# Scanning two states per instruction in a fused selective-scan and expert-FFN kernel

## Chip, cores and metric

The kernel runs on 1 core of one Trainium2 chip. The metric is the device time of one execution in microseconds; the median of several executions counts, lower is better.

## What is computed

For each of B=4 sequences of L=512 positions, with 512 channels and 16 states n, a selective scan is computed and added to x, and then a feed-forward part is added to that. Cut to what matters here (`silu`, the projections and the router left out):

```python
def step(state, inp):                      # over the 512 positions
    d, b, c, u = inp
    dA = jnp.exp(d[..., None] * A)         # [channel, state]
    state = state * dA + (d * u)[..., None] * b[:, None, :]
    y = jnp.einsum('bdn,bn->bd', state, c) # sum over the 16 states
    return (state, y)
...
y = y + D[None, :, None] * x
y = y * silu(z)                            # z = layernorm(x)
x = x + y
x = x + ffn(layernorm(x))                  # shared expert + top 2 of 16 experts
```

## The kernel before

One program with hand-placed instructions on five engines, ordered by semaphores. It has three stages. A preparation stage (to about 105 us) makes u, dt, B, C and silu(z) and stores them in scratch memory. The **scan stage** (105 to 580 us) is the one that the change touches. Then comes the routed part of the feed-forward, 47 units of 128 rows, which the change touches only in which PSUM banks some tiles have.

The scan stage has 16 **slots**: batch b = 0..3 times channel tile q = 0..3 (128 channels on partitions, 512 positions along the free dimension). Slots of batch 0 are written out; batches 1 to 3 are a loop of three turns whose body is the four slots. For each of the 16 states n a slot does:

- ScalarE (`decay`, L912): exp(dt*A[n]) into a PSUM bank of a ring of three, HS = banks 0 to 2; it waits until the bank is free (three states back).
- GpSimd (L1151): dbu = B * (dt*u), four states in one instruction of 2048 elements, made one slot ahead. dbu has one buffer, so each group of four waits for the scan of that group in the slot before.
- VectorE (`scan`, L1332): tensor_tensor_scan over the 512 positions, in place in the bank, or into h_p for the four states of POOL_N.
- product with C: on VectorE (`times_c`, L1346), bank to gs (ring of 6), for 12 states; on GpSimd (`times_c`, L1159), h_p to g_p, for the 4 states of POOL_N = (1, 5, 9, 13). VectorE's order is scan n, then the product of state n-1, so that between a scan and its product another scan runs.
- TensorE (`y_sum`, L615): turns the product (four 128x128 transposes) and adds it up in Y = bank 3, in the order of ORDER; the skip term m_du comes in the same way.

When the 16 states (and the skip term) of a slot are summed, VectorE multiplies Y with silu(z) into bank 7 (`take_y`, L1360, at state 2 of the next slot) and adds x (`gated`, L1367, at state 4); SyncE stores the result and at the end of a batch the rows are loaded again as xt.

Slots of batches 1 to 3 also carry one 128-row tile of the batch before through layernorm, router and shared expert ("rows"): `stats` on VectorE (L1374, at state 8 for q=0, 1 otherwise; three instructions that depend on each other), `rstd` on GpSimd (L1175), `xn` on ScalarE (L949), `xn_turn` on TensorE (L631, into TP = bank 7), `xnT_copy` on ScalarE (L955, after decay 15), `router` and the pieces of `shared` (L639, L647: 4+4 pieces of gate and up rows, 2 turns, 6 pieces of down), `gate` and `hT_copy` on ScalarE, `hidden` on VectorE (L1384), `swish` on GpSimd (L1169), `row_out` on ScalarE (L964). The tables at L41 to L52 say after which state each is issued; every engine takes its own instructions strictly in that order. GpSimd's slot is: m_w = dt*u, then four times (product with C of one state of the slot before, dbu of a group), swish after the first, rstd at the end.

Of the kernel before, what the change touches and what calls it, by code (L numbers as in the profile page):

```python
# [12 lines left out]
P = 128  # L13
# [41 lines left out]
def last_in_bank(k):  # L55

    if k >= RING_H:
        return k - RING_H
    return max(m for m in range(STEPS) if m % RING_H == k) - STEPS
# [12 lines left out]
def program(nc, x, ctxT, inT, convw, convb, xpT, dtT, dtb, alog, dskip, gateT, wgu, wdn, sgu, sdn, out):  # L72
# [11 lines left out]
    with ExitStack() as stack:  # L84
# [7 lines left out]
        bank = [stack.enter_context(nc.psum_tensor(f"bank{i}", [P, 512], F32)) for i in range(8)]  # L92
# [6 lines left out]
        TX, TH, ROUNDED = bank[3], bank[7], bank[0:3]  # L99
# [442 lines left out]
        def _(pe):  # L542
# [72 lines left out]
            def y_sum(b, q, m):  # L615

                i, n = b * DT + q, ORDER[m]
                if m == 0 and not (isinstance(i, int) and i < 1):
                    pe.wait_ge(y_taken, i)
                if m == SKIP_AT:  # L620
                    pe.wait_ge(du_ready, i + 1)
                    add_turned(m_du, False, False)
                if n in POOL_N:
                    pe.wait_ge(gp_ready, i * NP + by_pool(n) + 1)
                    tile = g_p[:, by_pool(n) % RING_P, :]
                else:
                    pe.wait_ge(g_ready, i * NV + by_vector(n) + 1)
# [3 lines left out]
            def xn_turn(j, x1_count):  # L631
                pe.wait_ge(xn_ready, j[0] + 1)
                pe.wait_ge(x1_ready, x1_count)
                pe.wait_ge(xnT_copied, 1 + j[0])
                for t in range(KH):
                    last = nc.tensor.transpose(TP[:, t * P:(t + 1) * P], f_xn[:, j[1] % 2, t * P:(t + 1) * P], ident[:])
                last.then_inc(xnT_ready, 1)
# [55 lines left out]
            def slot(b, q, rows):  # L693
# [12 lines left out]
                for n in range(NS):  # L706
                    y_sum(b, q, n)
                    for piece in early[PE_AT[n]:PE_AT[n + 1]] + late[LATE_AT[n]:LATE_AT[n + 1]]:
                        piece()
                    if rows and n == XN_TURN_AT[q > 0]:  # L710
                        xn_turn(f, i)
# [19 lines left out]
            for q in range(TB - 1):  # L731
                xn_turn((first + q, q), B * DT)
                router((first + q, q), first + q + 1, first + 2)
            whole((first + 2, 2), NT - 1)
            xn_turn((NT - 1, TB - 1), B * DT)
# [106 lines left out]
        def _(act):  # L842
# [69 lines left out]
            def decay(b, q, n):  # L912

                k = q * NS + n
                if not (isinstance(b, int) and b == 0 and k < RING_H):
                    m = last_in_bank(k)
                    if m % NS in POOL_N:
                        act.wait_ge(scan_done, b * STEPS + m + 1)
                    else:
                        act.wait_ge(g_ready, (b * DT + m // NS) * NV + by_vector(m % NS) + 1)  # L920
                if isinstance(b, int) and b == 0 and k == 2:
                    act.wait_ge(xd_copied, B)
                if n == 0:
                    act.wait_ge(d_loaded[q % 2], b * 32 + (q // 2) * 16 + 16)
                f(HS[k % RING_H][:], m_dt[:, q % 2, :], ACT.Exp, scale=c_a[:, q, n:n + 1]).then_inc(exp_done, 1)  # L925
# [29 lines left out]
            def xnT_copy(j, past):  # L955
                act.wait_ge(xnT_ready, 1 + j[0] + 1)
                act.wait_ge(down_ready, 1 + past)
                f(f_xnT[:, j[1], :], TP[:], ACT.Copy).then_inc(xnT_copied, 1)
# [9 lines left out]
            def slot(b, q, rows):  # L968
                j = ((b - 1) * DT + q, q)
                first = isinstance(b, int) and b == 0 and q == 0  # L970
                for n in range(NS):
# [24 lines left out]
                    if rows and n == XNT_AT[q > 0]:  # L996
                        xnT_copy(j, j[0])
# [21 lines left out]
            def xnT_of(q):  # L1019
                xnT_copy((first + q, q), first + q - 1)  # L1020
# [82 lines left out]
        def _(pool):  # L1103
# [28 lines left out]
            def slot(b, q, rows):  # L1132
# [7 lines left out]
                for gr in range(NG):  # L1140
# [3 lines left out]
                    else:  # L1144
                        times_c(*((b, q - 1) if q else (b - 1, DT - 1)), POOL_N[gr])
# [13 lines left out]
            def times_c(b, q, n):  # L1159

                i, at = b * DT + q, by_pool(n)
                pool.wait_ge(scan_done, i * NS + n + 1)
                pool.wait_ge(c_loaded[n // GRP], b * 16 + 16)
                if not (isinstance(i, int) and i == 0 and at < RING_P):
                    j, m = (i, POOL_N[at - RING_P]) if at >= RING_P else (i - 1, POOL_N[at - RING_P + NP])
                    pool.wait_ge(ymm_done, j * NS + ORDER.index(m) + 1)
                g.tensor_tensor(g_p[:, at % RING_P, :], h_p[:, at % RING_P, :], Cs[:, n, :], ALU.mult).then_inc(gp_ready, 1)  # L1167
# [21 lines left out]
            for n in POOL_N:  # L1189
                if n == POOL_N[SWISH_AFTER + 1]:  # L1190
# [68 lines left out]
        def _(dve):  # L1259
# [72 lines left out]
            def scan(b, q, n):  # L1332
                k = q * NS + n
                if n % GRP == 0:
                    dve.wait_ge(dbu_ready, (b * DT + q) * NG + n // GRP + 1)
                dve.wait_ge(exp_done, b * STEPS + k + 1)
                h = HS[k % RING_H][:]
                to = h
                if n in POOL_N:
                    i, at = b * DT + q, by_pool(n)  # L1340
                    if not (isinstance(i, int) and i == 0 and at < RING_P):
                        dve.wait_ge(gp_ready, i * NP + at - RING_P + 1)
# [3 lines left out]
            def times_c(b, q, n):  # L1346
                k, i, at = q * NS + n, b * DT + q, by_vector(n)
                dve.wait_ge(scan_done, b * STEPS + k + 1)
                if n % GRP == 0:
                    dve.wait_ge(c_loaded[n // GRP], b * 16 + 16)  # L1350
                if isinstance(i, int) and i == 0 and at < RING_G:
                    dve.wait_ge(z_turned, TB * (B - 1))
                    dve.wait_ge(dtp_ready, DT * (B if at >= RING_G - 2 else B - 1))
                else:

                    j, m = (i, DVE_N[at - RING_G]) if at >= RING_G else (i - 1, DVE_N[at - RING_G + NV])
                    dve.wait_ge(ymm_done, j * NS + ORDER.index(m) + 1)
                v.tensor_tensor(gs[:, (q * NV + at) % RING_G, :], HS[k % RING_H][:], Cs[:, n, :], ALU.mult).then_inc(g_ready, 1)  # L1358

            def take_y(b, i, q, copied):  # L1360

                dve.wait_ge(ymm_done, (i + 1) * NS)
                dve.wait_ge(xnT_copied, 1 + copied)
                dve.wait_ge(s_loaded[q % 2], b * 32 + (q // 2) * 16 + 16)
                v.tensor_tensor(TP[:], Y[:], m_szT[:, q % 2, :], ALU.mult).then_inc(y_taken, 1)

            def gated(b, i, q):  # L1367
# [4 lines left out]
                v.tensor_tensor(m_x[:, par], m_x[:, par], TP[:].rearrange("p (t j) -> p t j", t=TB), ALU.add).then_inc(x1_ready, 1)  # L1372

            def stats(j, jb):  # L1374
                at = j[1]
                dve.wait_ge(xt_loaded[at], jb * 16 + 16)
                v.bn_stats(f_st[:, at, :], xt[:, at, :]).then_inc(tstat_done, 1)
                dve.wait_ge(tstat_done, j[0] * 2 + 1)
                held(dve)
                v.bn_aggr(f_mv[:, at, :], f_st[:, at, :]).then_inc(tstat_done, 1)  # L1380
                dve.wait_ge(tstat_done, j[0] * 2 + 2)
                v.tensor_scalar(f_ve[:, at:at + 1], f_mv[:, at, 1:2], EPS, None, ALU.add).then_inc(var_ready, 1)

# [17 lines left out]

            def slot(b, q, rows):
                i = b * DT + q
                later = not (isinstance(b, int) and b == 0 and q == 0)
                j = ((b - 1) * DT + q, q)
                for n in range(NS):
                    scan(b, q, n)
                    if isinstance(b, int) and b == 0:
                        if q == 0 and n == SOFT_AT:
                            for k in range(DT):  # L1410
                                soft(B - 1, k)
                        if q == 0 and n in GAP_AT:
                            gap(B - 1, GAP_AT.index(n))
                        if q == 0 and n - 1 in GAP_AT:
                            total(B - 1, GAP_AT.index(n - 1))
                        if q == 2 and n == CLEAR_AT:
                            clear()
                    if n and n - 1 in DVE_N:
                        times_c(b, q, n - 1)
                    if n == TAKE_AT and later:  # L1420
                        take_y(*((b, i - 1, q - 1) if q else (b - 1, i - 1, DT - 1)), i - DT if rows else 0)
                    if n == GATED_AT and later:
                        gated(*((b, i - 1, q - 1) if q else (b - 1, i - 1, DT - 1)))
                    for c in range(2):
                        if n == HIDDEN_AT[c]:
# [4 lines left out]
                    if rows:  # L1430
                        if n == STATS_AT[q > 0]:
                            stats(j, b - 1)
                times_c(b, q, NS - 1)

            for q in range(DT):
# [4 lines left out]
            take_y(B - 1, B * DT - 1, DT - 1, NT - TB)  # L1440
# [9 lines left out]
            for q in range(TB - 1):  # L1450
                stats((first + q, q), B - 1)
            whole((first + 1, 1))
            stats((NT - 1, TB - 1), B - 1)
# [180 lines left out]
```

## Time and profile before

| | |
|---|---|
| runs | 1059.53, 1061.68, 1061.94 us; median 1061.68 us |
| profiled execution | 1053.36 us, its span 1051.6 us |
| busy over the span | PE 86%, DVE 79%, POOL 72%, ACT 49% |
| scan stage | about 105 to 580 us of the span |
| DVE in the scan stage | 28.8 of 29 us in most windows |
| TensorE's granted clock | 0.54 to 0.61 in the slots of batch 0, 1.00 in most of the loop |

The span runs from the first to the last instruction; the execution's own time is 1.8 us longer. In rows of the timeline the first number is the start, the second the duration, both in us; the difference between the starts of two neighbours is what the first one costs its engine.

### The profile page before, as it was taken

Reading aid. Unit: us, or ns where it says so; the run is one execution under the profiler, and the core shown is the slowest. Engines: PE = TensorE matmul, PEld = TensorE weight load, DVE = VectorE, ACT = ScalarE, POOL = GpSimd, SP = SyncE. Lnnn points to the kernel's source line nnn. Section 1 sums busy time; section 2 is a strip of 40 time slices with the busy share of each in tenths; the row PEclk is TensorE's granted clock in tenths of the full one; section 3 lists DMA queues with packets and bytes.
Section 4 is the critical chain, followed back from the end, with each engine's and each line's share of the span. In section 5 each row is a group of like instructions: output and inputs, shape, how many; then the busy total and the mean of one; then the engine's idle time right before and its main releaser. Section 6 shows DMA issues by size and latency. Waiting matters only on the chain.

```text
span 1051.6 us, 16598 instructions
## 1 busy us (share of the span) xinstructions
PE 899.8 (86%) x4352; PEld 653.7 (62%) x4353; DVE 828.9 (79%) x1349; ACT 517.5 (49%) x959; POOL 753.6 (72%) x482
## 2 busy tenths in 40 slices
PE   5876655689999789988999999869999999998993
PEld 2222334566665456655665555649998999887992
DVE  4788999999999899989999216768798989898000
ACT  3777634445655465555665222115554555454541
POOL 2436889899999799989993111027989888877872
PEclk9997656789999999999999989889999999999996
DMA  5568922562228322562210230134676777675432
GB/s 175 195 263 308 341 64 78 209 210 81 81 74 330 117 80 80 209 230 80 80 60 30 75 128 11 65 125 141 173 226 187 217 189 218 159 228 100 77 56 35
DMA packets 69987, 152.14 MB, mean 145 GB/s; under 512 B 7585, under 2 KB 23969, under 8 KB 64306
## 3 DMA queue, kind: packets, MB, share of 16 engines
q1 hardware_dynamic: 59410, 126.97, 35.2%
q0 software_dynamic: 10528, 24.65, 11.9%
q8 instruction: 14, 0.23, 0.1%
q14 instruction: 35, 0.29, 0.1%
HBM read 112.80 MB, written 38.80 MB: 144 GB/s over the span
## 4 chain that ended last, share of the span: by engine, by line
DVE 41%; PE 29%; issue 19%; DMA 3%; ACT 2%; DVEq 2%; POOL 1%; SPq 0%; POOLq 0%; ACTq 0%
DVE bank L1344 8%; PE bank L665 6%; DVE gs L1358 6%; PE bank L684 5%; DVE e_gu_lo L1571 4%; DVE e_gu_hi L1570 4%; PE bank L769 3%; PE bank L611 3%; PE bank L771 3%; DVE bank L1563 3%; PE bank L770 3%; DVE p_acc L1286 3%; DVE e_dn_lo L1571 2%; DVE e_dn_hi L1570 2%; DVE h_p L1344 2%
## 5 line engine op out<-in xcount | busy, mean ns | idle before, releaser
L1151 POOL TENSOR_TENSOR dbu<-bcs,m_w 128x2048 f32<-128x2048 f32 x64 | 296.1, 4627 | 11.4 <-DVE bank L1344 8.6
L925 ACT ACTIVATE bank<-m_dt,c_a 128x512 f32<-128x512 f32 x256 | 171.0, 686 | 196.8 <-DVE gs L1358 196.7
L1344 DVE TENSOR_TENSOR_SCAN bank<-bank,dbu 128x512 f32<-128x512 f32 x192 | 229.0, 1213 | 14.6 <-ACT bank L925 10.5
L611 PE MATMUL bank<-ident,gs 128*128 128x128 f32 x768 | 135.2, 307 | 70.0 <-DVE gs L1358 63.0
L665 PE MATMUL bank<-ws_gu,f_xnT 128*128 128x352 f32 x576 | 191.9, 474 | 2.8 <-ACT f_hT L947 1.9
L611 PEld LDWEIGHTS bank<-ident,gs 128*128 128x128 f32 x768 | 95.3, 154 | 129.5 <-DVE gs L1358 107.3
L665 PEld LDWEIGHTS bank<-ws_gu,f_xnT 128*128 128x128 f32 x576 | 106.2, 196 | 50.5 <-issue 5.3
L769 PE MATMUL bank<-e_gu_hi,e_xT_hi 128*128 x376 | 130.0, 346 | 4.0 <-DVEq L1585 3.1
L1358 DVE TENSOR_TENSOR gs<-bank,bcs 128x512 f32<-128x512 f32 x192 | 126.5, 665 | 0.0
L771 PE MATMUL bank<-e_gu_hi,e_xT_lo 128*128 x376 | 121.8, 324 | 0.0
L770 PE MATMUL bank<-e_gu_lo,e_xT_hi 128*128 x376 | 121.7, 324 | 0.0
L684 PE MATMUL bank<-ws_dn,f_hT 128*128 128x512 f32 (+1 forms) x216 | 107.3, 611 | 0.0
L1233 POOL DMA_INDIRECT out_rows<-e_y,t_tok x47 | 75.0, 1595 | 33.6 <-DMA out_rows<-e_y,t_tok 21.4
L1216 POOL TENSOR_TENSOR e_xT_lo<-e_xT,e_xT_hi 128x512 fp32r<-128x512 f32 x47 | 85.0, 1807 | 17.5 <-ACT e_xT_hi L1052 17.5
L1173 POOL TENSOR_TENSOR f_sg<-f_sg,f_g 128x352 f32<-128x352 f32 x36 | 33.7, 942 | 80.4 <-ACT f_sg L941 80.3
L1167 POOL TENSOR_TENSOR g_p<-h_p,bcs 128x512 f32<-128x512 f32 x64 | 81.6, 1274 | 10.0 <-DVE h_p L1344 6.3
L1563 DVE CAST bank<-e_gu 128x352 fp32r<-128x352 f32 x128 | 64.0, 521 | 22.7 <-issue 9.6
L1079 ACT ACTIVATE e_y<-bank,zero,t_w 128x512 f32<-128x512 f32 x47 | 36.7, 780 | 84.7 <-PE bank L771 83.0
L1344 DVE TENSOR_TENSOR_SCAN h_p<-bank,dbu 128x512 f32<-128x512 f32 x64 | 77.0, 1203 | 0.4 <-ACT bank L925 0.4
L769 PEld LDWEIGHTS bank<-e_gu_hi,e_xT_hi 128*128 128x128 f32 x376 | 71.3, 190 | 5.6 <-issue 5.6
L770 PEld LDWEIGHTS bank<-e_gu_lo,e_xT_hi 128*128 128x128 f32 x376 | 71.5, 190 | 0.0
L771 PEld LDWEIGHTS bank<-e_gu_hi,e_xT_lo 128*128 128x128 f32 x376 | 71.1, 189 | 0.0
(166 smaller groups left out, 1683.8 us busy)
## 6 DMA issues: line engine op xcount, KB each, us to landing
bcs<-bc_scratch SPq DMA_DIRECT2D x32, 1024.0 KB, 8.8
e_gu<-in_wgu SPq DMA_DIRECT2D x16, 1408.0 KB, 8.9
e_dn<-in_wdn SPq DMA_DIRECT2D x16, 512.0 KB
out_rows<-xt SPq DMA_DIRECT2D x18, 256.0 KB, 2.1
p_x<-in_x SPq DMA_DIRECT2D x4, 1024.0 KB, 7.0
u_scratch<-p_u SPq DMA_DIRECT2D x4, 1024.0 KB, 3.9
silu_z_scratch<-p_sz SPq DMA_DIRECT2D x4, 1024.0 KB, 5.0
dt_scratch<-p_dt SPq DMA_DIRECT2D x4, 1024.0 KB, 4.2
```

Source lines behind the costliest of these rows:

```text
L611: last = mm(Y[:, t * P:(t + 1) * P], tile[:, t * P:(t + 1) * P], ident[:], is_transpose=True, start=first and t == 0, stop=final and t == ...
L665: last = mm(dst[:, 0:I], lhs[t], ws_gu[:, t, off:off + I], start=t == 0, stop=t == KH - 1)
L684: last = mm(YO[:], f_hT[0:n, c, t, :], ws_dn[0:n, c, t, :], start=c == 0 and t == 0, stop=ends and not residual)
L769: mm(dst, a_hi, w_hi, start=first, stop=False)
L770: mm(dst, a_hi, w_lo, start=False, stop=False)
L771: return mm(dst, a_lo, w_hi, start=False, stop=final)
L925: f(HS[k % RING_H][:], m_dt[:, q % 2, :], ACT.Exp, scale=c_a[:, q, n:n + 1]).then_inc(exp_done, 1)
L1151: g.tensor_tensor(part_, Bs[:, gr * GRP:(gr + 1) * GRP, :], w, ALU.mult).then_inc(dbu_ready, 1)
L1216: g.tensor_tensor(e_xT_lo[:, par, :], e_xT[:], e_xT_hi[:, par, :].bitcast(F32), ALU.subtract).then_inc(xT_split, 1)
L1344: v.tensor_tensor_scan(to, h, dbu[:, n, :], 0.0, ALU.mult, ALU.add).then_inc(scan_done, 1)
L1358: v.tensor_tensor(gs[:, (q * NV + at) % RING_G, :], HS[k % RING_H][:], Cs[:, n, :], ALU.mult).then_inc(g_ready, 1)
L1563: v.tensor_copy(ROUNDED[(at + j) % 3][0:n, 0:w].bitcast(F32R), raw[0:n, t, c:c + w]).then_inc(rounded_done, 1)
```

## The change

States are handled in pairs p = (2p, 2p+1). HS gives way to PAIR, two pairs of neighbouring banks (0, 1 and 6, 7), used in turn. ScalarE fills a pair with two exps, the second without its first position, where a copy of one element writes 0, so that one scan of 1024 elements runs over both states. The product with C takes the pair in one instruction too, directly behind its scan. POOL_N is (2, 3, 10, 11), two whole pairs; GpSimd's product is one instruction of 1024 elements. Slot (0, 0) keeps the states one by one. `take_y` writes in place into Y, so the next slot's sums wait for `gated` (x1_ready). YO moves to bank 2 (and the rows that `xn_turn` turns go there, in the loop), one ROUNDED buffer to bank 6. The places of nearly all side instructions move.

```diff
-POOL_N = (1, 5, 9, 13)
+POOL_N = (2, 3, 10, 11)
-ORDER = (0, 2, 3, 1, 4, 6, 7, 5, 8, 10, 11, 9, 12, 14, 15, 13)
+ORDER = (0, 1, 4, 5, 2, 3, 6, 7, 8, 9, 12, 13, 10, 11, 14, 15)
+PAIRS = NS // 2
-PE_AT = (3, 3, 4, 4, 5, 5, 6, 6, 7, 7, 8, 8, 9, 9, 9, 10, 10)
-LATE_AT = (0, 0, 0, 1, 1, 2, 2, 3, 3, 5, 5, 6, 6, 6, 6, 6, 6)
-XN_TURN_AT = (12, 9)
-GATE_AT, HT_AT, XN_AT, XNT_AT = (6, 8), 2, (14, 10), (15, 15)
-TAKE_AT, LOGITS_AT, GATED_AT, HIDDEN_AT, STATS_AT, ADD_AT = 2, 5, 4, (9, 13), (8, 1), 15
+PE_AT = (4, 4, 4, 4, 4, 4, 4, 5, 6, 7, 8, 8, 9, 9, 9, 9, 10)
+LATE_AT = (0, 1, 2, 3, 4, 5, 6, 6, 6, 6, 6, 6, 6, 6, 6, 6, 6)
+XN_TURN_AT = (12, 11)
+GATE_AT, HT_AT, XN_AT, XNT_AT = (5, 7), 1, (14, 10), (15, 15)
+LOGITS_AT, HIDDEN_AT, STATS_AT, ADD_AT = 3, (5, 6), (4, 0), 13
...
-        HS, Y, GU, YO, TP = bank[0:3], bank[3], bank[4:6], bank[6], bank[7]
+        HS, Y, GU, YO, TP = bank[0:3], bank[3], bank[4:6], bank[2], bank[7]
+        PAIR = (banks[:, 0:2, :], banks[:, 6:8, :])
...
             def y_sum(b, q, m):
-                    pe.wait_ge(y_taken, i)
+                    pe.wait_ge(x1_ready, i)
...
             def decay(b, q, n):
+                if n % 2 == 0:
+                    j, m = (i, n - 4) if p > 1 else (i - 1, n + NS - 4)
+                    if isinstance(i, int) and i == 1 and p < 2:
+                        act.wait_ge(g_ready, NV)
+                        act.wait_ge(dt_ready, B * DT)
+                    elif m in POOL_N:
+                        act.wait_ge(scan_done, j * NS + m + 2)
+                    else:
+                        act.wait_ge(g_ready, j * NV + by_vector(m) + 2)
+                    f(PAIR[p % 2][:, 0, :], m_dt[:, q % 2, :], ACT.Exp, scale=c_a[:, q, n:n + 1]).then_inc(exp_done, 1)
+                else:
+                    f(PAIR[p % 2][:, 1, 0:1], zero[:], ACT.Copy)
+                    f(PAIR[p % 2][:, 1, 1:L], m_dt[:, q % 2, 1:L], ACT.Exp, scale=c_a[:, q, n:n + 1]).then_inc(exp_done, 1)
...
+            def scan_pair(b, q, p):
+                if n % GRP == 0:
+                    dve.wait_ge(dbu_ready, i * NG + n // GRP + 1)
+                dve.wait_ge(exp_done, i * NS + n + 2)
...
+                if n in POOL_N:
+                    dve.wait_ge(gp_ready, i * NP + by_pool(n))
+                    to = h_p[:].rearrange("p n l -> p (n l)")
+                w = dbu[:, n:n + 2, :].rearrange("p n l -> p (n l)")
+                v.tensor_tensor_scan(to, h, w, 0.0, ALU.mult, ALU.add).then_inc(scan_done, 2)
+
+            def pair_times_c(b, q, p):
+                dve.wait_ge(scan_done, i * NS + n + 2)
+                if n % GRP == 0:
+                    dve.wait_ge(c_loaded[n // GRP], b * 16 + 16)
+                j, m = (i, DVE_N[at + 1 - RING_G]) if at >= RING_G else (i - 1, DVE_N[at + 1 - RING_G + NV])
+                dve.wait_ge(ymm_done, j * NS + ORDER.index(m) + 1)
+                v.tensor_tensor(gs[:, g:g + 2, :], PAIR[p % 2], Cs[:, n:n + 2, :], ALU.mult).then_inc(g_ready, 2)
...
             def slot(b, q, rows):
+                for p in range(PAIRS):
+                    scan_pair(b, q, p)
+                    if not rows and p == 0:
+                        take_y(*past)
+                    if rows and p == STATS_AT[q > 0]:
+                        stats(j, b - 1)
...
+                        if p == HIDDEN_AT[c]:
...
+                    if 2 * p in DVE_N:
+                        pair_times_c(b, q, p)
+                    if rows and p == 0:
+                        take_y(*past)
+                    if rows and p == STATS_AT[q > 0]:
+                        spread(j)
+                    if p == 0:
+                        gated(*past)
+                    if rows and q and p == STATS_AT[1]:
+                        variance(j)
+                    if rows and q == 0 and p == STATS_AT[0] + 1:
+                        variance(j)
```

## Rows read from the trace of the kernel before

**Rows 1.** The page, part 1: busy time and share by engine.
```profile
PE 899.8 (86%) x4352; PEld 653.7 (62%) x4353; DVE 828.9 (79%) x1349; ACT 517.5 (49%) x959; POOL 753.6 (72%) x482
```

**Rows 2.** Windows of 29 us: busy by engine, granted clock, DMA share, GB/s.
```profile
309.00:338.00 29.00, 26.81 (x135) 17.51 (x134) 28.81 (x36) 16.66 (x32) 27.95 (x14) 1.00 0.80 281
```

**Rows 3.** Timeline of DVE over one slot of the loop.
```profile
301.57 0.50 DVE L1388 TENSOR_TENSOR f_h<-f_sg,bank 128x352 f32<-128x352 f32 x1
...
304.24 0.67 DVE L1358 TENSOR_TENSOR gs<-bank,bcs 128x512 f32<-128x512 f32 x1
304.83 1.21 DVE L1344 TENSOR_TENSOR_SCAN bank<-bank,dbu 128x512 f32<-128x512 f32 x1
305.96 0.67 DVE L1358 TENSOR_TENSOR gs<-bank,bcs 128x512 f32<-128x512 f32 x1
...
314.95 0.67 DVE L1377 BATCH_NORM_STATS2 f_st<-xt 128x6 f32<-128x512 f32 x1
315.77 0.18 DVE L1380 BATCH_NORM_AGGREGATE f_mv<-f_st 128x2 f32<-128x6 f32 x1 [0.15 <-DVE f_st L1377]
...
316.08 1.23 DVE L1344 TENSOR_TENSOR_SCAN bank<-bank,dbu 128x512 f32<-128x512 f32 x1
...
329.81 0.51 DVE L1388 TENSOR_TENSOR f_h<-f_sg,bank 128x352 f32<-128x352 f32 x1
```

**Rows 4.** Groups of DVE by shape: busy, mean ns of one, idle before.
```profile
L1344 DVE TENSOR_TENSOR_SCAN bank<-bank,dbu 128x512 f32<-128x512 f32 x192 | 229.0, 1213 | 14.6 <-ACT bank L925 10.5 <-issue 4.1
L1358 DVE TENSOR_TENSOR gs<-bank,bcs 128x512 f32<-128x512 f32 x192 | 126.5, 665 | 0.0
...
L1538 DVE TENSOR_TENSOR dbu<-iota_row,r_r 128x1024 f32<-128x1024 f32 x4 | 4.6, 1220 | 0.0
...
L1493 DVE TENSOR_TENSOR_SCAN r_inc<-r_res,r_tot 128x256 f32<-128x256 f32 x1 | 0.7, 691 | 0.0
```

**Rows 5.** Timeline of DVE in the preparation stage, around 43 us.
```profile
42.39 0.68 DVE L1293 SCALAR_TENSOR_TENSOR p_dt<-bank,p_e 128x512 f32<-128x512 f32 x1
43.11 0.69 DVE L1295 TENSOR_SCALAR bank<-p_e 128x512 f32<-128x512 f32 x1
43.71 0.68 DVE L1293 SCALAR_TENSOR_TENSOR p_dt<-bank,p_e 128x512 f32<-128x512 f32 x1
```

**Rows 6.** Line L1357, DVE's sequencer: ns min/median/max, first and last start.
```profile
L1357 DVEq ALU_OP  x141: 40/40/40, 229.6 to 575.8; - x141
```

**Rows 7.** Timeline of PE in the same slot.
```profile
307.19 0.60 PE L636 MATMUL bank<-ident,f_xn 128*128 128x128 f32 x4
307.62 0.60 PE L611 MATMUL bank<-ident,gs 128*128 128x128 f32 x4
...
314.32 3.80 PE L665 MATMUL bank<-ws_gu,f_xnT 128*128 128x352 f32 x12
...
321.87 1.02 PE L684 MATMUL bank<-ws_dn,f_hT 128*128 128x512 f32 x2
```

**Rows 8.** Timeline of ACT in the same slot.
```profile
310.47 0.59 ACT L958 ACTIVATE f_xnT<-bank 128x512 f32<-128x512 f32 x1
310.95 1.99 ACT L925 ACTIVATE bank<-m_dt,c_a 128x512 f32<-128x512 f32 x3
...
320.27 0.16 ACT L962 ACTIVATE logits<-bank 128x16 f32 x1
```

**Rows 9.** Timeline of POOL in the same slot.
```profile
304.79 1.27 POOL L1167 TENSOR_TENSOR g_p<-h_p,bcs 128x512 f32<-128x512 f32 x1
306.02 4.62 POOL L1151 TENSOR_TENSOR dbu<-bcs,m_w 128x2048 f32<-128x2048 f32 x1
...
317.89 1.26 POOL L1138 TENSOR_TENSOR m_w<-m_u,m_dt 128x512 f32<-128x512 f32 x1 [0.45 <-DMA m_u<-u_scratch]
319.54 1.27 POOL L1167 TENSOR_TENSOR g_p<-h_p,bcs 128x512 f32<-128x512 f32 x1 [0.39 <-POOL m_w L1138]
```

**Rows 10.** Timeline of DVE: `stats` of q=0 in the loop's second turn.
```profile
361.17 0.69 DVE L1377 BATCH_NORM_STATS2 f_st<-xt 128x6 f32<-128x512 f32 x1 [1.75 <-DMA xt<-x_scratch]
```

More of the change, by code:

```diff
@@ L731, in _ @@
             for q in range(TB - 1):
-                xn_turn((first + q, q), B * DT)
+                xn_turn((first + q, q), TP, None)
                 router((first + q, q), first + q + 1, first + 2)
             whole((first + 2, 2), NT - 1)
-            xn_turn((NT - 1, TB - 1), B * DT)
+            xn_turn((NT - 1, TB - 1), TP, None)
             router((NT - 1, TB - 1), NT, NT - 1)
@@ L953, in xn, with xnT_copy @@
                 f(f_xn[:, j[1] % 2, :], xt[:, j[1], :], ACT.Identity, scale=f_rs[:, j[1]:j[1] + 1], bias=f_nm[:, j[1]:j[1] + 1]).then_inc(xn_ready, 1)
-            def xnT_copy(j, past):
+            def xnT_copy(j, past, turned):
                 act.wait_ge(xnT_ready, 1 + j[0] + 1)
                 act.wait_ge(down_ready, 1 + past)
-                f(f_xnT[:, j[1], :], TP[:], ACT.Copy).then_inc(xnT_copied, 1)
+                f(f_xnT[:, j[1], :], turned[:], ACT.Copy).then_inc(xnT_copied, 1)
             def lg_copy(fx):
@@ L1019, in xnT_of @@
             def xnT_of(q):
-                xnT_copy((first + q, q), first + q - 1)
+                xnT_copy((first + q, q), first + q - 1, TP)
             xn_of(0)
@@ L1188, in _ @@
             first = NT - TB
-            for n in POOL_N:
-                if n == POOL_N[SWISH_AFTER + 1]:
+            for n in POOL_N[0::2]:
+                if n == POOL_N[2]:
                     swish((first, 0))
@@ L1380, in stats, with variance, row_stats @@
                 v.bn_aggr(f_mv[:, at, :], f_st[:, at, :]).then_inc(tstat_done, 1)
+            def variance(j):
+                at = j[1]
                 dve.wait_ge(tstat_done, j[0] * 2 + 2)
                 v.tensor_scalar(f_ve[:, at:at + 1], f_mv[:, at, 1:2], EPS, None, ALU.add).then_inc(var_ready, 1)
+            def row_stats(j):
+                stats(j, B - 1)
+                spread(j)
+                variance(j)
             def hidden(f, c):
@@ L1400, in clear, with slot_by_state @@
                 v.memset(f_xnT[:, 2:4, :], 0.0).then_inc(dummy_ready, 1)
+            def slot_by_state():
+                for n in range(NS):
+                    scan(n)
+                    if n == SOFT_AT:
+                        for k in range(DT):
+                            soft(B - 1, k)
+                    if n in GAP_AT:
+                        gap(B - 1, GAP_AT.index(n))
+                    if n - 1 in GAP_AT:
+                        total(B - 1, GAP_AT.index(n - 1))
+                    if n and n - 1 in DVE_N:
+                        times_c(n - 1)
+                times_c(NS - 1)
             def slot(b, q, rows):
                 i = b * DT + q
-                later = not (isinstance(b, int) and b == 0 and q == 0)
                 j = ((b - 1) * DT + q, q)
[L1406 to L1423, printed above, removed]
+                past = (b, i - 1, q - 1) if q else (b - 1, i - 1, DT - 1)
+                for p in range(PAIRS):
[4 more added lines that the diff above has]
+                        stats(j, b - 1)
+                    if not rows and q == 2 and 2 * p == CLEAR_AT:
+                        clear()
                     for c in range(2):
-                        if n == HIDDEN_AT[c]:
+                        if p == HIDDEN_AT[c]:
                             if rows:
@@ L1429, in slot @@
                                 hidden((0, 0), c)
[L1430 to L1435, printed above, removed]
+                    if 2 * p in DVE_N:
[3 more added lines that the diff above has]
+                    if rows and p == STATS_AT[q > 0]:
+                        spread(j)
+                    if p == 0:
[3 more added lines that the diff above has]
+                    if rows and q == 0 and p == STATS_AT[0] + 1:
+                        variance(j)
+            slot_by_state()
+            for q in range(1, DT):
                 slot(0, q, False)
@@ L1450, in _ @@
             for q in range(TB - 1):
-                stats((first + q, q), B - 1)
+                row_stats((first + q, q))
             whole((first + 1, 1))
-            stats((NT - 1, TB - 1), B - 1)
+            row_stats((NT - 1, TB - 1))
             whole((first + 2, 2))
```

106 lines of the change are left out of this document (57 added, 49 removed).

## The prediction

> **What bounds the kernel now.** The page's part 1 gives no answer by itself: TensorE has the largest share [rows 1], but most of it falls in the expert stage, which the change doesn't reach. So I read the scan stage by windows. There VectorE is busy 28.81 of 29 us, GpSimd 27.95, TensorE 26.81, ScalarE 16.66 [rows 2]: VectorE has no room, and GpSimd hardly any. The groups say the same: before 192 scans VectorE sat idle 14.6 us in all, before 192 products 0.0 [rows 4]. So a slot takes what VectorE's instructions cost from start to start. From `hidden` to the same `hidden` a slot later it is 329.81 - 301.57 = 28.24 us [rows 3].
>
> What one instruction costs is the distance to the next start, not its duration: a scan of 1.21 us costs 305.96 - 304.83 = 1.13 us, a product of 0.67 costs 0.59 [rows 3]. Neighbours overlap by some 0.08 us when the second doesn't depend on the first. Check: 16 x 1.13 + 12 x 0.59 + `take_y` and `gated` (as a product) 1.18 + two `hidden` of 352 elements 0.86 + the `stats` block 316.08 - 314.95 = 1.13 gives 28.3.
>
> **Fewer instructions on VectorE.** A scan of 256 elements takes 691 ns, one of 512 takes 1213 [rows 4]: 512 more elements are 1.04 us, so a pair costs 1.13 + 1.04 = 2.17 us. A product of 1024 elements takes 1220 ns against 665 [rows 4], so a pair costs 0.59 + 0.555 = 1.14. A slot saves 8 x (2.26 - 2.17) + 6 x (1.18 - 1.14) = 0.72 + 0.24 = 0.96 us, and not the whole fixed part of each duration, since the overlap hides most of that already.
>
> **A new dependence.** The product now stands right behind its own scan; before, another scan lay between. What does VectorE lose on an instruction that waits for its neighbour? Two rows bound it. In the preparation L1295 waits for L1293: start to start 0.72 us, and the next, independent one, 0.60 [rows 5]: 0.12. In `stats` the aggregation waits and the sequencer does one more step between wait and start: 0.82 us, where an independent one costs 0.58: 0.24 [rows 3]. The product has such a step: an address operation of 40 ns for its second wait (L1357, x141) [rows 6], which can't run before the first wait is over; where n is a multiple of 4 a third wait comes on top. I take 0.26, and 0.33 with the third wait, since the second row is nearest; bounds 0.12 and 0.40. `stats` or `hidden` stands between for p=0 and p=6 (q>0) or p=4 and p=6 (q=0). Exposed in a loop slot: two of each kind, 2 x 0.26 + 2 x 0.33 = 1.18 us. In the three pair slots of batch 0 five are exposed (p=2, 3, 4, 6, 7): 1.51 us.
>
> **Stats taken apart.** The block of 1.13 becomes 0.58 + 0.10 + 0.07 = 0.75 us, since other work lies between its parts: 0.38 saved. With q=0 `gated` now stands right behind `take_y`: 0.2 lost.
>
> VectorE's own sum of a loop slot: 28.24 - 0.96 - 0.38 + 1.18 = 28.08, for q=0 28.28.
>
> **A wait that comes closer.** `xnT_copy` sits in ScalarE's queue after decay 15, ahead of the two exps that the next slot begins with, and it waits for `xn_turn`, which now comes after the sums of states 12 and 13, that is after the product of pair 6. Count from the start of that product. It ends at 1.22. TensorE: two sums of 0.43 [rows 7], `turn(0)` of three transposes 0.33 (estimate, three quarters of four), then `xn_turn` of 0.60: done at 3.1. ScalarE: the copy costs 310.95 - 310.47 = 0.48 [rows 8], an exp about 0.65, the one-element copy between 0.1 and 0.2 (a row of 16 elements takes 0.16 [rows 8]), the last exp ends after 0.69 and I allow 0.05 for each wake-up: the pair is ready at 5.15. VectorE would come to it at 1.14 + 2.17 + 0.26 + 1.14 = 4.71. So it waits 0.44 us a slot. Before, the copy waited too, but the ring of three banks and the earlier turn left room: three exps follow the copy at once [rows 8]. For q=0 `xn_turn` comes one sum later: 0.87 us. Behind that wait stand only the exps; who waits for them is VectorE.
>
> **TensorE, and the other waits.** Per slot its work is 17 sums of 0.43, 16 gate and up matmuls at 3.80 / 6 = 0.63, 7 down matmuls at about 0.86 [rows 7], turns and router about 2: 25.4 us. It is not the bound, but from the product of pair 2 to that of pair 6 it must do sums, four down pieces and four up pieces, about 13.0 us against 13.4 of VectorE, so it arrives about when it is needed. The sums of a new slot now wait for `gated`, some 5 us into it; TensorE has router and four pieces first (6 us), so I cost that at nothing. `take_y` follows the last product by 3.3 us and two sums take 1.1: nothing. With batch 0's lower clock two sums cost perhaps twice that, still under a pair scan.
>
> **GpSimd.** Busy 27.95 of 29 us [rows 2], that is 27.2 of a slot of 28.24; the waits on its own results (0.39 behind m_w [rows 9] and about 0.2 in rstd) make 27.8, and 0.45 of DMA wait may go. Of its product 1.23 us for 512 elements and of dbu 4.6 for 2048 [rows 9] make 2.35 for a pair: two save 0.2. It can't go below 27.6. Its variance comes at about 5.4 us of a slot instead of 3.9; GpSimd then waits for it up to 1 us, and has that much.
>
> **Moved loads.** `gated` of q=0 comes some 4 us earlier, and with it the store and reload of x1; `stats` then stands later. The stall of 1.75 us before it [rows 10] goes, taken as 1.6 in each of three turns. Next late there is nothing: `stats` comes over 1 us later and its data 4 us earlier, more than the stall was. The idle time at the loop's turn I leave as it is; the branch stays. Slot (0, 1) begins with exps that wait for the last product of slot (0, 0): 1.5 us, once (two exps and wake-ups).
>
> **The sum.** Nine loop slots with q>0: 28.08 + 0.44 - 28.24 = +0.28, times 9 = +2.5. Three with q=0: 28.28 + 0.87 - 28.24 - 1.6 = -0.7, times 3 = -2.1. Three of batch 0: -0.96 + 1.51 = +0.55, times 3 = +1.6. Joining: +1.5. Together +3.5 us on the profiled execution of 1053.36 us, so 1056.9. The median of the runs shown is 8.3 us above that execution; I add the difference to the median: 1065.
>
> **Rivals.**
>
> 1. *The dependence is cheap.* If it costs 0.12 each, a loop slot has 27.4 us on VectorE, GpSimd's 27.6 comes first, with part of the ScalarE wait on top 27.8: 9 x -0.44, q=0 3 x -1.6, batch 0 3 x -0.36, joining +1.5: -8.5 us, 1053. For it speaks that [rows 5] is a real pair with 0.12. Against it, the extra step [rows 3, 6].
>
> 2. *Merging saves the whole fixed time.* By durations a pair scan saves 2 x 1213 - 2257 = 169 ns, a pair product 110, and dependence costs nothing: 2.0 us a slot. Then GpSimd is the bound in every slot: 9 x -0.7, 3 x -2, 3 x -1.5, +1.5: -15 us, 1046.5. The overlap between starts [rows 3] speaks against it. It is what the Trainium skill's page "VectorE: DVE Perf Modes", section "The DRAIN you can't avoid", would have: the next instruction starts only when the pipe is empty, a semaphore costs nothing extra, so one should lower the count of instructions. By that rule, the trace doesn't agree: 0.60 without a wait and 0.72 with one [rows 5].
>
> 3. *The turned rows hold up the exps (slower).* Place: the one sketched above. It decides as soon as TensorE comes to the sum of state 12 later than the product of pair 6. It has 0.4 us of room there; one up piece (1.25 us) late in its queue, or later norm rows, passes through to VectorE in full. With 0.5 to 1 us more in each of 12 slots: +6 to +12 on top of +3.5, so 1071 to 1077, 1073 the middle. For it speaks TensorE's 26.81 of 29 [rows 2]; against it that ScalarE is half idle and that pieces were moved out of the slot's end.
>
> 4. *GpSimd decides anyway.* If its phase, now tied to the variance and to scans of pairs, sets 28.2 a slot, gain and loss on VectorE vanish: 1061, no change.
>
> **Chances.** The forecast 0.38: its values lie from 1062 to 1068, nearly half of them within 0.3% (3.2 us, about what a measurement of this kernel can tell from no change), the rest above. Rival 1: 0.20. Rival 2: 0.07. Rival 3: 0.23. Rival 4: 0.12. So faster 0.27, same 0.28, slower 0.45. The range goes from just under rival 1 to the upper part of rival 3: 1052 to 1076; outside lie rival 2 and the end of rival 3. Around the forecast alone it would be 1061 to 1069.
>
> **What would show it.** Pair scans near 2.26 us and products near 1.22; idle of 0.15 to 0.25 before products of p=2, 3, 4, 7, released by the scan; 0.3 to 1 us idle before the first scan of each loop slot, released by ScalarE's exp, which itself waited behind f_xnT; no DMA wait before `stats`; GpSimd over 27 of 28.5 us. The prediction is wrong if that idle time before products is under 0.08 or over 0.3, if the first scan waits over 1 us, or if an engine other than VectorE sets the slot.

## The result, and the profile after

The changed kernel takes 1076.09 us (median of 4 runs, 1067.62 to 1076.98) against 1060.61 us before on the same chip. The ratio, which goes by the means of the runs (1074.20 and 1060.26 us) and not by the medians, is 1.0131, 95% interval 1.0076 to 1.0187: slower by 1.3%, or about 14 us. The profiled execution took 1076.08 us, 22.7 us more than that of before. The forecast was +3.5 us.

The page after, parts 1 and 3; against [rows 1] VectorE has 210 instructions less and is busy 3.4 us less, in a span 22.8 us longer:

```profile
span 1074.4 us, 16127 instructions
...
PE 890.2 (83%) x4352; PEld 657.9 (61%) x4353; DVE 825.5 (77%) x1139; ACT 523.6 (49%) x1079; POOL 748.7 (70%) x450
...
q14 instruction: 24, 0.20, 0.1%
```

The groups of VectorE after, by shape (as [rows 4]):

```profile
L1387 DVE TENSOR_TENSOR_SCAN banks<-banks,dbu 128x1024 f32<-128x1024 f32 x90 | 205.8, 2287 | 7.5 <-ACT banks L940 7.5
L1399 DVE TENSOR_TENSOR gs<-banks,bcs 128x1024 f32<-128x1024 f32 x90 | 109.9, 1221 | 6.9 <-DVE banks L1387 1.9 <-PE banks L607 0.2
...
L1439 DVE TENSOR_TENSOR f_h<-f_sg,banks 128x352 f32<-128x352 f32 x36 | 18.6, 519 | 42.5 <-issue 20.6 <-POOL f_sg L1189 13.7 <-PE banks L666 7.8
...
L1417 DVE BATCH_NORM_STATS2 f_st<-xt 128x6 f32<-128x512 f32 x16 | 10.8, 674 | 7.8 <-DMA xt<-x_scratch 7.8
```

The third line has the loss: before `hidden` VectorE is idle 42.5 us, of which 23.6 us fall in the scan stage, in 22 waits. Before the change the same group (L1388) had 17.4 us, all after the scan stage. Over the loop (from 260 us on), VectorE's waits are these, first before the change, then after (us in total, times, longest):

```profile
DVE bank L1344 <- issue: 4.1, 1, 4.1
DVE f_st L1377 <- DMA xt<-x_scratch: 3.0, 2, 1.7
DVE bank L1344 <- ACT bank L925: 2.9, 1, 2.9
DVE f_mv L1380 <- DVE f_st L1377: 1.5, 10, 0.2
```

```profile
DVE f_h L1439 <- issue: 19.7, 17, 2.1
DVE banks L1387 <- ACT banks L940: 5.1, 10, 0.8
DVE f_h L1439 <- PE banks L666: 2.9, 3, 1.0
DVE gs L1399 <- DVE banks L1387: 1.4, 6, 0.3
```

Three old waits are gone: those for the reloaded rows, those inside `stats`, and, not forecast, the idle time at the two places where the loop goes back to its start, its turns (4.1 and 2.9 us). One new wait outweighs them. Most of it stands under "issue", that is, the profile names no releaser; the timelines of VectorE and TensorE name it. VectorE, one slot of the loop:

```profile
324.09 2.28 DVE L1387 TENSOR_TENSOR_SCAN h_p<-banks,dbu 128x1024 f32<-128x1024 f32 x1
326.28 2.27 DVE L1387 TENSOR_TENSOR_SCAN banks<-banks,dbu 128x1024 f32<-128x1024 f32 x1
328.65 1.22 DVE L1399 TENSOR_TENSOR gs<-banks,bcs 128x1024 f32<-128x1024 f32 x1
329.79 2.29 DVE L1387 TENSOR_TENSOR_SCAN banks<-banks,dbu 128x1024 f32<-128x1024 f32 x1
...
336.83 2.28 DVE L1387 TENSOR_TENSOR_SCAN h_p<-banks,dbu 128x1024 f32<-128x1024 f32 x1
341.22 0.52 DVE L1439 TENSOR_TENSOR f_h<-f_sg,banks 128x352 f32<-128x352 f32 x1 [2.11 <-issue]
341.66 2.29 DVE L1387 TENSOR_TENSOR_SCAN banks<-banks,dbu 128x1024 f32<-128x1024 f32 x1
344.90 0.52 DVE L1439 TENSOR_TENSOR f_h<-f_sg,banks 128x352 f32<-128x352 f32 x1 [0.95 <-issue]
```

TensorE in the same slot:

```profile
329.93 0.66 PE L607 MATMUL banks<-ident,gs 128*128 128x128 f32 x4 [1.85 <-DVE gs L1399]
...
332.30 1.91 PE L685 MATMUL banks<-ws_dn,f_hT 128*128 128x512 f32 x2
...
339.78 1.35 PE L666 MATMUL banks<-ws_gu,f_xnT 128*128 128x352 f32 x4
...
343.46 1.35 PE L666 MATMUL banks<-ws_gu,f_xnT 128*128 128x352 f32 x4
```

The up pieces (L666) end at 341.13 and 344.81, and the two `hidden` start at 341.22 and 344.90: each waits for its up piece. TensorE does those pieces only after the sums of states 7 and 9, and it had waited 1.85 us itself for the product of pair 2. In this slot it then also lost speed: two down matmuls took 1.91 us, usually 1.02 [rows 7]. The granted clock says why (windows of 2 us; columns as in [rows 2], the clock is the third number from the end); it stands at full level, falls to half and comes back:

```profile
328.00:330.00 2.00, 0.15 (x2) 0.08 (x2) 1.91 (x3) 1.12 (x4) 2.00 (x2) 1.00 0.12 43
330.00:332.00 2.00, 2.00 (x9) 1.30 (x10) 2.00 (x1) 1.30 (x3) 2.00 (x1) 0.78 0.02 5
332.00:334.00 2.00, 2.00 (x5) 0.87 (x4) 1.91 (x3) 0.57 (x1) 2.00 (x1) 0.50 0.88 289
334.00:336.00 2.00, 2.00 (x12) 1.46 (x11) 1.91 (x2) 1.52 (x4) 2.00 (x4) 0.87 0.75 299
```

What the three windows lack of the full clock (0.22, 0.50 and 0.13 of 2 us) is 1.7 us, so the clock stood at half for 3.4 us. In slots without such a fall the first wait is 0.43 us instead of 2.11, and a slot takes 30.0 us instead of 31.7. Before it was 28.24. The fall came in five of the twelve loop slots: 5 x 1.68 = 8.4 us of the 23.6.

### The profile page after: what moved, and what is told of

It reads as the page before. It is cut to its first block and busy times, and to the rows that moved or that the text cites. A ratio compares the mean times of both kernels' runs of the same rounds, so it can differ in the third digit from the quotient of the medians.

```text
span 1074.4 us, 16127 instructions
## 1 busy us (share of the span) xinstructions
PE 890.2 (83%) x4352; PEld 657.9 (61%) x4353; DVE 825.5 (77%) x1139; ACT 523.6 (49%) x1079; POOL 748.7 (70%) x450
## 5 line engine op out<-in xcount | busy, mean ns | idle before, releaser
L1387 DVE TENSOR_TENSOR_SCAN banks<-banks,dbu 128x1024 f32<-128x1024 f32 x90 | 205.8, 2287 | 7.5 <-ACT banks L940 7.5
L607 PE MATMUL banks<-ident,gs 128*128 128x128 f32 x768 | 124.4, 300 | 102.6 <-DVE gs L1399 82.5
L607 PEld LDWEIGHTS banks<-ident,gs 128*128 128x128 f32 x768 | 98.5, 153 | 159.2 <-DVE gs L1399 105.6
L666 PE MATMUL banks<-ws_gu,f_xnT 128*128 128x352 f32 x576 | 189.7, 474 | 1.4 <-ACT f_g L954 1.4
L666 PEld LDWEIGHTS banks<-ws_gu,f_xnT 128*128 128x128 f32 x576 | 107.7, 197 | 51.3 <-issue 5.2
L770 PE MATMUL banks<-e_gu_hi,e_xT_hi 128*128 x376 | 130.1, 346 | 4.5 <-POOL e_xT_lo L1232 2.3
L772 PE MATMUL banks<-e_gu_hi,e_xT_lo 128*128 x376 | 122.1, 325 | 0.0
L771 PE MATMUL banks<-e_gu_lo,e_xT_hi 128*128 x376 | 122.0, 324 | 0.0
L1399 DVE TENSOR_TENSOR gs<-banks,bcs 128x1024 f32<-128x1024 f32 x90 | 109.9, 1221 | 6.9 <-DVE banks L1387 1.9
L685 PE MATMUL banks<-ws_dn,f_hT 128*128 128x512 f32 (+1 forms) x216 | 115.1, 640 | 0.0
L1094 ACT ACTIVATE e_y<-banks,zero,t_w 128x512 f32<-128x512 f32 x47 | 36.6, 779 | 84.5 <-PE banks L772 82.6
```

The costliest lines, as they stand in the source:

```text
L607: last = mm(Y[:, t * P:(t + 1) * P], tile[:, t * P:(t + 1) * P], ident[:], is_transpose=True, start=first and t == 0, stop=final and t == ...
L666: last = mm(dst[:, 0:I], lhs[t], ws_gu[:, t, off:off + I], start=t == 0, stop=t == KH - 1)
L685: last = mm(YO[:], f_hT[0:n, c, t, :], ws_dn[0:n, c, t, :], start=c == 0 and t == 0, stop=ends and not residual)
L770: mm(dst, a_hi, w_hi, start=first, stop=False)
L771: mm(dst, a_hi, w_lo, start=False, stop=False)
L772: return mm(dst, a_lo, w_hi, start=False, stop=final)
```

## Experiments

All are compared with the kernel before on the same chip; e1 to e4, e5 to e8 and e9 to e11 ran together, each group on a chip of its own. Between groups, and against the changed kernel, "by the ratios" is the difference of the two ratios times 1060 us.

**e1: `hidden` one pair later.**

```diff
-LOGITS_AT, HIDDEN_AT, STATS_AT, ADD_AT = 3, (5, 6), (4, 0), 13
+LOGITS_AT, HIDDEN_AT, STATS_AT, ADD_AT = 3, (6, 7), (4, 0), 13
```

> The changed kernel with both `hidden` products one pair later (HIDDEN_AT 6, 7 in place of 5, 6). Theory A: the loss is VectorE waiting in its own queue, at `hidden`, for the up pieces that TensorE gets to only after the sums of states 6 to 9. The idle time before f_h in the loop, about 25 us together, goes; 0.4 to 0.9 us before each first scan stays. 22 to 25 us less than the changed kernel, a slot of 28.4 us, close to or just below the kernel before. Theory B: TensorE is simply full, and the wait moves to the next place that needs it (the turned rows, take_y, ring of gs): at most 8 us less. Either way no idle time at the turn of the loop.

Measured: 1045.33 us, ratio 0.9869 (0.9827 to 0.9910). The edit of two digits turns the change from 1.3% slower into 1.3% faster. VectorE's waits over the loop:

```profile
DVE banks L1387 <- ACT banks L940: 5.9, 10, 1.8
DVE gs L1399 <- DVE banks L1387: 1.4, 6, 0.3
```

No wait before f_h is left in the loop, and TensorE keeps up: theory A. By the medians, which are from different chips, the gain is 31 us; by the ratios it is 28, and from the first `take_y` to the last of the profiled executions also 27.8 us (450.8 to 423.0), where at most 25 were expected. The waits make 23.6 us. About 2 more come from the overlap of 0.09 us between neighbours that each of the 22 waits had cost. And 12 x 0.18 = 2.2 come from a dependence that is no longer exposed: the second `hidden` now stands between the scan and the product of pair 7 (for the 0.18 see e3). Half clock still struck twice in this loop, and two waits before a first scan were 1.7 and 1.8 us; in most other slots that wait was 0.2.

**e2: the turned rows earlier.**

```diff
-XN_TURN_AT = (12, 11)
+XN_TURN_AT = (11, 9)
```

> The changed kernel with xn_turn after sums 11 and 9 in place of 12 and 11, nothing else. Theory A: the idle time before the first scan of a slot (0.41, for q=0 0.85 us, released by the exp) comes from xnT_copy in front of the exps; it goes, 12 times, 5 to 7 us less than the changed kernel; the waits at `hidden` stay as they are. Theory B: the exps are late for another reason (ScalarE's own work, the free pair): unchanged time.

Measured: 1061.68 us, ratio 1.0036 (1.0014 to 1.0059): by the ratios 10 us less than the changed kernel. The waits before the first scan of a slot are nearly gone (5.1 us before, 0.7 now, from 260 us on), so `xnT_copy` ahead of the exps was their cause, as forecast. It gave more than expected; in the profiled execution the waits of 2.11 us had become 0.43, since the clock's fall no longer struck there.

**e3: both edits.**

> Both edits. If the two waits are separate, their gains add: 27 to 32 us less than the changed kernel, a slot of about 28.0 us (VectorE's own sum), some 10 us faster than the kernel before. If TensorE's total work is the limit, it stays within 3 us of the first one.

Measured: 1042.29 us, ratio 0.9859 (0.9823 to 0.9896), the lowest of the study: 1.4% faster than before. e3 and e1 differ by 3 us, less than the two gains added, and their intervals overlap, so the totals don't tell them apart. In the traces e3 is 4.0 us shorter from the first `take_y` to the last: from 260 us on VectorE waits for exps four times, 3.0 us in all, where in e1 it waited ten times, 5.9 us. Half clock struck in e3 too, twice in the loop, behind idle times of TensorE of 1.9 and 2.0 us, for 6.8 us each time, and the slots behind took 28.57 us instead of 27.72: only 0.85 us was lost, where 3.4 us of half clock cost the changed kernel 1.7. And in two slots with q=0 the wait, of 0.8 and 0.9 us, lies before a later scan, whose exp stands behind `xn`, which waits for GpSimd. Its VectorE timeline (the slot from `take_y` at 286.59 to 314.31, 27.7 us) shows no idle time but 0.09 us before each of three products:

```profile
290.18 2.27 DVE L1387 TENSOR_TENSOR_SCAN banks<-banks,dbu 128x1024 f32<-128x1024 f32 x1
292.54 1.23 DVE L1399 TENSOR_TENSOR gs<-banks,bcs 128x1024 f32<-128x1024 f32 x1
293.68 2.29 DVE L1387 TENSOR_TENSOR_SCAN banks<-banks,dbu 128x1024 f32<-128x1024 f32 x1
...
302.92 2.27 DVE L1387 TENSOR_TENSOR_SCAN banks<-banks,dbu 128x1024 f32<-128x1024 f32 x1
305.10 0.51 DVE L1439 TENSOR_TENSOR f_h<-f_sg,banks 128x352 f32<-128x352 f32 x1
305.53 1.21 DVE L1399 TENSOR_TENSOR gs<-banks,bcs 128x1024 f32<-128x1024 f32 x1
```

A scan followed by its own product costs 2.36 us (290.18 to 292.54), one of the same duration followed by something else 2.18 (302.92 to 305.10): the dependence costs 0.18 us.

**e7 and e8: what merging saves.** On e3, the pair scan as two scans (e7), the pair product as two products (e8):

```diff
-                v.tensor_tensor_scan(to, h, w, 0.0, ALU.mult, ALU.add).then_inc(scan_done, 2)
+                for c in (0, L):
+                    v.tensor_tensor_scan(to[:, c:c + L], h[:, c:c + L], w[:, c:c + L], 0.0, ALU.mult, ALU.add).then_inc(scan_done, 1)
```

```diff
-                v.tensor_tensor(gs[:, g:g + 2, :], PAIR[p % 2], Cs[:, n:n + 2, :], ALU.mult).then_inc(g_ready, 2)
+                for c in range(2):
+                    v.tensor_tensor(gs[:, g + c, :], PAIR[p % 2][:, c, :], Cs[:, n + c, :], ALU.mult).then_inc(g_ready, 1)
```

> e3 (both waits removed) with the pair scan split into two scans of 512, each with its own increment; product still of the pair. Two scans cost 2 x 1.13 = 2.26 us from start to start against 2.20 measured for the pair. By the overlap between neighbours: +0.06 x 8 pairs x 15 slots, 6 to 8 us more than e3. If merging saved the whole fixed time of a scan (0.17 us by durations): 20 us more.

> e3 with the pair product split into two of 512. By start to start: 2 x 0.59 against 1.14, +0.04 x 6 x 15 = 3 to 4 us more than e3; TensorE gets the first half 0.5 us earlier, which may give some back. If merging saved the whole fixed time (0.11 us by durations): 10 us more.

Measured: e7 1049.31 us, ratio 0.9902 (0.9869 to 0.9934); e8 1046.31 us, ratio 0.9889 (0.9819 to 0.9959). By the medians, from another chip than e3's, that is 7.0 and 4.0 us more than e3, by the ratios 4.6 and 3.2, and neither interval is clear of e3's. The traces are sharper: a slot without waits takes 28.10 us in e7 and 27.93 in e8 against 27.72, so merging saves 0.38 us a slot on the scans and 0.21 on the products, 0.6 in all; 0.96 was forecast. It is small, near what starts show, and far from the 2.0 us that durations suggest.

**e4, e5, e6: the turn of the loop.** Why did 7 us at the turns go? Three kernels move or lengthen VectorE's program with semaphore increments, which cost its data path nothing: with them a loop slot takes 30.03 us in e4 as in the changed kernel, and with none in the loop 28.25 in e5 against 28.24. e4: the changed kernel with 4 behind each pair scan in the loop; e6: the same and one behind each pair scan of slots (0,1) to (0,3); e5: the kernel before with two behind each scan of those slots:

```diff
                 for n in range(NS):
                     scan(b, q, n)
+                    if not rows and q:
+                        held(dve)
+                        held(dve)
```

> The changed kernel with four semaphore increments behind each pair scan of the loop (128 in its body, made while the scan runs, so free of cost on the data path). VectorE's loop body grows from about 240 to about 368 instructions; before the change it had 340. Theory A: the idle time of 4.1 and 2.9 us at the loop's two turns, gone in the changed kernel, was the fetch of instructions for a body that is too long to stay in the engine's buffer: it comes back, 5 to 8 us more, and instruction packets appear again between 330 and 560 us. Theory B: the idle time came from something that the change reordered (waits across the turn): it stays gone and the time stays within 1 us.

> The kernel before with 96 semaphore increments in VectorE's program ahead of its loop (two behind each scan of slots (0,1) to (0,3), in the loop nothing). The body stays at about 340 instructions but begins 96 later. The fetches of 128 instructions that belong to VectorE fall at its instructions 330, 458, 586 and 714 (counted in the trace, within 10); the body runs from 383 to 725 and so lies in four such blocks and crosses 714. Moved by 96 it lies in three. Theory A (the loop's turn fetches its first block again when the body crossed into a fourth): the idle time of 4.1 and 2.9 us at the turns goes, and with it the instruction packets between 340 and 560 us; about 7 us less than the kernel before. Theory B (the idle time belongs to waits across the turn): unchanged, ratio 1.000.

> The long body of e4 (128 increments in the loop, 367 instructions) moved by 24 more increments ahead of the loop. There it ran from 337 to 704, short of 714; here it ends at 728 and crosses. Theory A: instruction packets and idle time at the turns of the loop appear, 3 to 4 us each, so 5 to 8 us more than e4, unless the waits of the first pair cover part. Theory B: as e4.

e4 took 1074.26 us, ratio 1.0180 (1.0124 to 1.0236); no stall at the turns and no instruction packet there (none between 320 and 590 us): the theory that the length of the body decides fell. I then counted VectorE's instructions in the trace up to each instruction packet, and that gave the theory of e5 and e6. e5: 1051.45 us, ratio 0.9946 (0.9913 to 0.9978), 0.5% (5.7 us) faster than the kernel before by the place of its loop alone, 7 us being expected. The two slots with a turn shrank by 3.2 and 2.1 us; a wait of 0.8 us for ScalarE's exp stands there now, which the stall had hidden. The pages' instruction queue, e5 and then e6:

```profile
q14 instruction: 26, 0.21, 0.1%
```

```profile
q14 instruction: 35, 0.29, 0.1%
```

With e5 the count falls from 35 (as counted on the page before) to 26. In e6 it is 35 where e4 has 25, and both turns stall again:

```profile
350.26 2.30 DVE L1387 TENSOR_TENSOR_SCAN banks<-banks,dbu 128x1024 f32<-128x1024 f32 x1 [3.40 <-ACT banks L937]
...
475.88 2.30 DVE L1387 TENSOR_TENSOR_SCAN banks<-banks,dbu 128x1024 f32<-128x1024 f32 x1 [2.22 <-issue]
```

In e4 these two waits were 0.47 and 0.46. The total of e6, 1075.36 us, ratio 1.0150 (1.0083 to 1.0217), doesn't separate it from e4; the traces do. The last `take_y` comes at 600.5 us against 594.5.

**e9, e10, e11: the first wait and the clock.** e9 moves only the second `hidden` (HIDDEN_AT = (5, 7)). e10 is the changed kernel with the down pieces forward, e11 is e3 with the same edit:

```diff
-LATE_AT = (0, 1, 2, 3, 4, 5, 6, 6, 6, 6, 6, 6, 6, 6, 6, 6, 6)
+LATE_AT = (0, 1, 3, 4, 5, 6, 6, 6, 6, 6, 6, 6, 6, 6, 6, 6, 6)
```

> The changed kernel with only the second `hidden` one pair later (HIDDEN_AT 5, 7). If the two waits at `hidden` are separate, the 0.95 us of the second goes and the first (0.43, or 2.1 us in slots where TensorE's clock falls) stays: 9 x 0.95 and somewhat more, 9 to 14 us less than the changed kernel. If the first wait is only what is left of one lag of TensorE, the first grows and little is won: under 4 us.

> The changed kernel with the down pieces pulled one place forward (two behind the second sum in place of one), so that TensorE's wait of 1.85 us for the product of pair 2 shrinks to about 1.0 and the up pieces come 0.9 us sooner. Theory A (TensorE's queue between pair 2 and the up pieces is the chain, and its idle time there is what half clock follows): the waits of 0.43 go, 0.95 stays or shrinks, 2.1 us waits no longer appear: 10 to 16 us less than the changed kernel. Theory B (the up pieces wait for ScalarE's gates or for the sums, not for the down pieces): within 3 us of it.

> e3 with the same down pieces pulled forward. The slots of e3 are at VectorE's own sum (27.7 us) already; only what is left before the first scan (0.6 to 0.9 us in four slots) can go: 0 to 4 us less than e3.

e9: 1052.32 us, ratio 0.9943 (0.9918 to 0.9969). e10: 1056.88 us, ratio 0.9998 (0.9972 to 1.0024). e11: 1045.22 us, ratio 0.9872 (0.9830 to 0.9913), no gain on e3. In e9 the first wait stays at 0.43 and the second is gone; in e10 the first is gone and the second is 0.63, with TensorE's own wait down from 1.85 to 0.99 us:

```profile
276.74 0.52 DVE L1439 TENSOR_TENSOR f_h<-f_sg,banks 128x352 f32<-128x352 f32 x1 [0.43 <-issue]
```

```profile
327.02 0.65 PE L607 MATMUL banks<-ident,gs 128*128 128x128 f32 x4 [0.99 <-DVE gs L1399]
```

```profile
310.28 0.52 DVE L1439 TENSOR_TENSOR f_h<-f_sg,banks 128x352 f32<-128x352 f32 x1 [0.63 <-issue]
```

So two orders that must agree disagreed, TensorE's and VectorE's, and either can be moved; moving VectorE's costs nothing, and it is the better cure. By the ratios e9 gained 20 us and e10 14. e9 is above its forecast of 9 to 14: the second waits were 11 us, but of the five first waits of 2.1 us only one is left, which gives 6.7 more, and 2.5 went before the first scans. The one that is left:

```profile
393.80 0.52 DVE L1439 TENSOR_TENSOR f_h<-f_sg,banks 128x352 f32<-128x352 f32 x1 [2.11 <-issue]
```

## Why the prediction was partly right

The side was right, slower being the likeliest outcome, and 1076 us lies at the very edge of the range. The size was not: 3.5 us forecast, about 14 by the ratio. And of its own signs of being wrong one came true, that another engine than VectorE sets the slot: TensorE held VectorE up at `hidden` for 0.9 to 3.1 us in each of the twelve loop slots.

**The step that failed** is "TensorE, and the other waits". It set TensorE's work between the products of pair 2 and pair 6 (13.0 us) against VectorE's (13.4), found that it "arrives about when it is needed", and charged nothing. It asked when the *sum* of state 12 is needed. But the up pieces lie ahead of that in the same queue, and their reader, `hidden`, stands in VectorE's queue at pairs 5 and 6, up to 3 us earlier. What the traces show in its place: from the product of pair 2 to the second up piece TensorE has 9.5 us of work at full clock (11.20 in the slot shown, less 1.7), VectorE comes to `hidden` after 9.2, and the second `hidden` comes after 2.7 us more, while TensorE needs 3.7. That is 0.43 and 0.95 us a slot, put at nothing, and 23.6 us in all with the falls of the clock; e1 takes it away. The costs of the pieces were in the text; their consumer was not looked up. Rival 3 had the mechanism, TensorE late by a piece passing through to VectorE, and its size (1071 to 1077), but at the wrong place, behind the turned rows; e1 shows the place. What remains unforeseen in kind is the half clock, 1.7 us in each of the five slots where it struck.

**Point by point.** The pair scan costs 2.18 to 2.20 us from start to start (forecast 2.17), the pair product 1.14 (1.14). The dependence costs 0.18 us (taken 0.26 and 0.33; nearer to rival 1's 0.12): 1.18 forecast for the four of a slot, 0.7 measured. The idle time before those products, 0.09 us, lies outside the 0.15 to 0.25 forecast, just above the 0.08 named as a sign of being wrong. With q>0 and in batch 0 the third wait added nothing. With q=0 the dependence cost more: VectorE was idle 0.32 us before the product of pair 0 and 0.19 before those of pairs 2 and 3, where it was 0.09 elsewhere; why is open. VectorE's own sum of a slot was put at 28.08 us, and the trace gives about 28.0 (30.03 less the waits and the overlap that they cost). That agreement is luck: merging saved 0.4 us less than forecast (0.6 for 0.96), and the dependence cost 0.5 less. The wait before the first scan was 0.41 us and 0.85 for q=0, against 0.44 and 0.87 forecast, with the cause shown by e2. The stall before `stats` went, as forecast (4.7 us in the three turns, 4.8 forecast). Joining slot (0, 1) cost 1.60 us (1.5). The three pair slots of batch 0 took 83.7 us from `take_y` to `take_y` against 82.6 (1.1 more; 1.6 forecast). GpSimd never set the slot of the changed kernel: rival 4 fell, and even e3's slot of 27.7 us, close to the 27.6 forecast as GpSimd's floor, has no wait of VectorE for it. GpSimd did wait longer for the variance than I had allowed (2.48 us against 1). The table ahead of the prediction gives TensorE a clock of 0.54 to 0.61 in batch 0; the fourth slot (199 to 227 us) had 0.93. No term rests on that.

**The turn of the loop** was left "as it is; the branch stays". That was wrong in the change's favour: 7 us of idle time, worth 5 to 6 us by e5. Without it the loss would have been about 1.8% and the time outside the range; that it stands at the edge is luck, since this gain was in no term.

**Rival 2** falls by e7 and e8. The Trainium skill, page "VectorE: DVE Perf Modes", section "The DRAIN you can't avoid", says that a semaphore between neighbours costs nothing extra; here it costs 0.18 us (2.36 against 2.18), and the time by that rule, rival 2's 1046.5 us, lies 30 us under the one measured.

Put together along the profiled executions, from `take_y` to `take_y`: batch 0 +1.1 us; the loop up to its last slot +14.2 (324.2 to 338.5, rounded); the last slot +3.9 (24.7 to 28.6). All after the scan stage took 473.2 us before and 477.1 after; the other kernels show 472.6 to 480.5 there, so these 3.9 us of the 22.8 lie within the spread between executions, and the ratio of 1.3% is the figure to hold on to.

## What to carry to other kernels

When instructions are regrouped on the bounding engine, go through every instruction in its queue, the small side jobs too, and ask at what moment the other engine delivers its input; two in-order queues stall each other wherever one's order of consumption doesn't match the other's order of production, and the side job costs as much as the main one. Merging two instructions on VectorE is worth what the distances between starts show (here 0.05 us for two scans of 512, 0.04 for two products), less 0.18 us wherever an instruction then stands right behind the one that it depends on. And look at idle time where a loop turns before crediting or debiting it to an edit: it may depend on where the body lies in the program.

## What the runs showed of the hardware

**Instruction fetch at a loop's turn.** In the later turns of the loop one packet of VectorE's instructions comes every 126 to 132 executed ones (before, e6), so they come in blocks of 128. A body of 340 instructions that touched four of these blocks and crossed into the fourth was fetched anew at each turn and stalled 4.1 and 2.9 us; moved by 96 instructions it wasn't, and a body of 367 stalled or not according to 24 instructions ahead of it (e6, e4); e5 and e4 touch three blocks, before and e6 four. The Trainium skill, page "Runtime: NRT & Kernel Launch", section "Instruction fetch mechanics", says that a taken branch whose target has left the two-page window stalls for a fetch. The stall agrees; its figure of 512 instructions in two blocks of 256 doesn't fit packets 128 instructions apart, and the measurement decides. How many blocks are held was not measured by itself.

**TensorE's clock** fell to half for 3.4 us at a time in five loop slots of the changed kernel. Ahead of each fall TensorE had been idle while it waited for the product of pair 2: 2.29 us in the three slots with q=1, and 1.85 us in two others. The slot with q=1 in the loop's second turn:

```profile
392.04 0.69 PE L607 MATMUL banks<-ident,gs 128*128 128x128 f32 x4 [2.29 <-DVE gs L1399]
392.54 1.91 PE L685 MATMUL banks<-ws_dn,f_hT 96*128 96x512 f32 x2
```

In four other slots an idle time of 1.85 us brought no fall, in e4 one of the three of 2.29 brought none, and in e1 one of 2.87 brought none. In e2 the idle times at that place were 1.86 us once and then at most 1.6, and no fall came in the loop; in e10 they were at most 1.44, and none came either. So the falls go with the longer idle times, and what decides in the single slot stays open.
